# Attention batches of a register loop written out one behind the other

## What is computed

```python
xn = _layernorm(x)                                   # (8, 1024, 256)
Q, K = xn @ Wq, xn @ Wk                              # 16 heads x 2 x 16
V = xn @ Wv                                          # 16 heads x 16
A1 = einsum('bhqd,bhkd->bhqk', Q1, K1) * scaling
A2 = einsum('bhqd,bhkd->bhqk', Q2, K2) * scaling
attn = softmax(A1) - lamb * softmax(A2)
out = einsum('bhqk,bhkd->bhqd', attn, V) @ Wo        # then layer norm, gamma, beta
...
return x + attention(xn) + feed_forward_attention(xn)
```

## Time and profile before

| what | before |
|---|---|
| median of three runs | 4403.33 us |
| the profiled execution | 4398.99 us |
| its span | 4397.2 us |
| TensorE busy | 3937.4 us (90%) |
| VectorE busy | 3106.2 us (71%) |
| ScalarE busy | 2852.8 us (65%) |
| GpSimd busy | 1330.7 us (30%) |
| instructions in the trace | 76116 |
| mean granted TensorE clock | 0.936 |

### The profile page before, as it was taken

How to read it: one execution, slowest core, us unless ns; L and a number is a source line. 1 busy time by engine, 2 the same in 40 slices (tenths; PEclk the granted TensorE clock), 3 DMA queues, 4 the chain that set the end, 5 groups by cost and what they waited for, 6 DMA issues and landing times. The chain is left out here.

```text
span 4397.2 us, 76116 instructions
## 1 busy us (share of the span) xinstructions
PE 3937.4 (90%) x23970; PEld 1611.4 (37%) x23970; DVE 3106.2 (71%) x5547; ACT 2852.8 (65%) x3429; POOL 1330.7 (30%) x1618
## 2 busy tenths in 40 slices
PE   4489999999999999999999999999999477779999
PEld 2123223232322332332223223232322144458888
DVE  3567997888789789878987997888796122234444
ACT  0007887888788788878887887888889444422221
POOL 4211421242142123313221421342141344464330
PEclk7669999999999999999999999999999787789999
DMA  9610211111111111111111111111110366543220
GB/s 317 240 58 28 66 35 50 35 54 45 35 56 62 40 40 54 40 45 40 64 53 32 64 35 50 35 54 52 45 56 24 122 194 200 180 132 96 92 82 20
DMA packets 224807, 332.04 MB, mean 76 GB/s; under 512 B 29297, under 2 KB 165236, under 8 KB 219780
## 3 DMA queue, kind: packets, MB, share of 16 engines
q1 hardware_dynamic: 205956, 276.47, 19.3%
q0 software_dynamic: 18432, 50.36, 3.5%
HBM read 169.34 MB, written 156.34 MB: 74 GB/s over the span
## 5 line engine op out<-in xcount | busy, mean ns | idle before, releaser
L1514 DVE TENSOR_REDUCE arena<-psum 128x1 f32<-128x512 f32 x4096 | 2596.9, 683 | 474.9 <-PE psum L1087 438.8
L1318 ACT ACTIVATE arena<-psum,arena 128x1024 f32<-128x1024 f32 x2048 | 2163.0, 1111 | 193.4 <-PE psum L1125 170.3
L1087 PE MATMUL psum<-arena 48*128 48x512 f16 x4096 | 1383.6, 394 | 80.3 <-DVE arena L1514 22.3
L1141 PE MATMUL psum<-arena 128*32 128x512 f32 x8200 | 1107.3, 612 | 1.4 <-ACT arena L1242 0.7
L1087 PEld LDWEIGHTS psum<-arena 48*128 48x128 f16 x4096 | 322.9, 93 | 1645.0 <-DVE arena L1514 1115.5
L1125 PE MATMUL psum<-arena 50*128 50x512 f16 x4096 | 876.4, 383 | 52.2 <-issue 29.6
L1380 POOL TENSOR_TENSOR arena<-arena 128x16 f32<-128x16 f32 x129 | 28.8, 223 | 1775.6 <-DVE arena L1524 1775.6
L566 DVE TENSOR_TENSOR leaf_arena<-psum,leaf_arena 128x256 f32<-128x256 f32 x240 | 90.7, 420 | 314.8 <-PE psum L510 314.8
L1073 PE MATMUL psum<-arena 128*128 128x256 f32 x1024 | 289.8, 408 | 11.0 <-DVE arena L1514 11.0
L747 ACT ACTIVATE mix_arena<-psum,mix_arena 128x1024 f32<-128x1024 f32 x64 | 71.4, 1115 | 321.9 <-DVE mix_arena L767 321.8
L1125 PEld LDWEIGHTS psum<-arena 50*128 50x128 f16 x4096 | 210.1, 94 | 168.6 <-ACT arena L1318 90.1
(11 more groups left out here) (165 smaller groups left out, 3202.4 us busy)
## 6 DMA issues: line engine op xcount, KB each, us to landing
arena<-scratch_split SPq DMA_DIRECT2D x768, 64.0 KB, 2.1
scratch_split<-arena SPq DMA_DIRECT2D x64, 512.0 KB, 3.2
scratch_sorted_x<-route_arena SPq DMA_DIRECT2D x60, 512.0 KB, 8.1
leaf_arena<-scratch_sorted_x SPq DMA_DIRECT2D x60, 512.0 KB, 4.8
scratch_sorted_y<-leaf_arena SPq DMA_DIRECT2D x60, 512.0 KB, 3.2
leaf_arena<-in_leafw SPq DMA_DIRECT2D x3, 5128.0 KB, 19.2
arena<-in_x SPq DMA_DIRECT2D x18, 512.0 KB, 4.3
scratch_sum<-arena SPq DMA_DIRECT2D x18, 512.0 KB, 3.0
```

The source lines that it names most:

```text
L1087: nc.tensor.matmul(aux_bank[bank], ring[at, slot, 0, m, qt * P:(qt + 1) * P], ring[at, slot, 1, m, c * CH:(c + 1) * CH], start=True, stop=True
L1141: last = nc.tensor.matmul(value_bank[32 * j:32 * j + 32, :], vaug[:, kt, 2 * (s % PER_BATCH) + j % 2, :], prob[:, step % 2, j, :], start=k ...
L1318: nc.scalar.activation(prob[:, step % 2, 2 * h:2 * h + 2, :], score[:, 2 * h:2 * h + 2, :], ACT.Exp, scale=exp_scale[:, s % 2, s // 2:s // ...
L1514: nc.vector.tensor_reduce(halfmax[:, odd, 2 * m + h, qt, c:c + 1], aux_bank[bank], AX.X, ALU.max).then_inc(bank_used[bank], 1)
```

## The change

In each of the five engines' programs the hardware loop and the tail are replaced by a loop of the generating program over eight constants, so that eight bodies are written out one behind the other. The register that held a snapshot of the output group's number on SyncE goes away. Three waits that asked whether their number was a constant now ask whether it is above zero. They stand for the same waits as before: none at the first use, and the same count at every later one. The order of the work on each engine stays as it was.

```diff
--- before.py
+++ after.py
@@ -1021,8 +1021,6 @@
 
                 batch = (i + LAST) % BATCH
                 group = [2 * batch, 2 * batch + 1]
-                if not tail:
-                    group = [sp.snap(group[0]), sp.snap(group[1])]
                 for s in range(PER_BATCH):
 
                     if s % 2 == 0:
@@ -1051,9 +1049,8 @@
                         sp.wait_ge(scattered, i * (16 * TT * NFFF) + 16 * TT * NFFF)
                         load_rows(i + 1)
 
-            with sp.Fori(0, LAST) as i:
-                body(i, False)
-            body(LAST, True)
+            for i in range(BATCH):
+                body(i, i == LAST)
             for h in range(2):
                 sp.wait_ge(groups[h].y_ready, BATCH + 1)
                 groups[h].load(nc.sync, w["x"], 2 * LAST + h)
@@ -1215,9 +1212,8 @@
                             use(i, k + n, s, *todo[n], tail)
                         k += len(todo)
 
-            with pe.Fori(0, LAST) as i:
-                body(i, False)
-            body(LAST, True)
+            for i in range(BATCH):
+                body(i, i == LAST)
             values(LAST, PER_BATCH - 1, STEPS - 1)
             for n, (kind, number) in enumerate(EPILOGUE):
                 bank, turn = bank_use(TAIL + n)
@@ -1244,7 +1240,7 @@
             def read_qk(t, tile, number, bank):
 
                 a, c = number // (QK_UNITS // 2), number % (QK_UNITS // 2)
-                if not (isinstance(t, int) and t == 0):
+                if t > 0:
 
                     act.wait_ge(split_ready, t * 4 + (number // 2 - 3))
                 nc.scalar.activation(rest[:, a, c * QW:(c + 1) * QW], aux_bank[bank][:, 0:QW], ACT.Identity,
@@ -1255,7 +1251,7 @@
                 nc.scalar.activation(vaug[:, tt, :, 0:HD], src, ACT.Copy).then_inc(bank_used[bank], 1)
 
             def read_shift(n, bank):
-                if not (isinstance(n, int) and n == 0):
+                if n > 0:
 
                     act.wait_ge(shift_in, n * 64)
                 nc.scalar.activation(mrow[0:2 * PARTS, :], aux_half[bank][0:2 * PARTS, :], ACT.Copy).then_inc(bank_used[bank], 1)
@@ -1332,9 +1328,8 @@
                             if (s, step) == (1, 2 if h == 0 else 15):
                                 groups[h].guess_std(nc, act, i)
 
-            with act.Fori(0, LAST) as i:
-                body(i, False)
-            body(LAST, True)
+            for i in range(BATCH):
+                body(i, i == LAST)
             copy_values(LAST, PER_BATCH - 1, 1)
             for n, (kind, number) in enumerate(EPILOGUE):
                 act.wait_ge(extra_full, LAST * ITER_EXTRAS + (PRO_EXTRAS + TAIL_EXTRAS + n + 1))
@@ -1352,11 +1347,9 @@
 
                 a, c = number // 2, number % 2
                 cols = slice(c * CH, (c + 1) * CH)
-                if number == 0 and not isinstance(t, int):
+                if number == 0 and t > 0:
 
                     pool.wait_ge(split_stored, t * 32)
-                if isinstance(t, int) and t == 1 and number == 0:
-                    pool.wait_ge(split_stored, 32)
                 nc.gpsimd.tensor_tensor(split[:, a, 0, cols], rest[:, a, cols], zeros[:, 0:CH], ALU.add
                                         ).then_inc(pchain, 1)
                 pool.wait_ge(pchain, t * 4 + (number + 1))
@@ -1426,9 +1419,8 @@
                         for n in range(4 * (s - 1), 4 * s):
                             scatter(n // NFFF, n % NFFF)
 
-            with pool.Fori(0, LAST) as i:
-                body(i, False)
-            body(LAST, True)
+            for i in range(BATCH):
+                body(i, i == LAST)
             join_maps(BATCH * 2 * PER_BATCH, PER_BATCH - 1, 1)
             for h in range(2):
                 groups[h].finish(nc, pool, BATCH)
@@ -1564,9 +1556,8 @@
                             if (s, step) == (1 + h, 4):
                                 groups[h].inverse_std(nc, dve, link, i)
 
-            with dve.Fori(0, LAST) as i:
-                body(i, False)
-            body(LAST, True)
+            for i in range(BATCH):
+                body(i, i == LAST)
             link = Chain(dve, dchain, BATCH * per_iter + links_before)
             wait_read(dve, LAST, TAIL + EPILOGUE.index(("o", 1)))
             invert(1)
```

## The result

The changed kernel takes 4336.47 us in the median of four runs (4331.39 to 4351.24), the kernel before 4404.18 (4395.32 to 4408.93). The ratio is 0.9859, with a 95% interval of 0.9838 to 0.988. The profiled execution takes 4334.91 us, 64.1 less than the profiled one before.

A forecast was written before the change was run, and what follows sets the result against it. TensorE, busy 3937.4 of 4397.2 us, was taken as the bound, VectorE and ScalarE close behind in attention. Savings 50.7 + 6.3 + 4.2 + 2.4 = 63.6 us from 4398.99 gave 4335.4, written 4336; range 4322 to 4348, chance 0.80.

The forecast's parts named there:

- Taken branches: Seams between batches: six taken branches cost 8.45 us each in idle time and lowered clock, 50.7 us saved.
- step 4: Sets 3, 5 and 7 of seven batches: 0.20 us less each without register instructions, 4.2 us saved.
- Set 0 of batch 0: First set, no branch in front: the clock stays low from the stage's start, so nothing credited.
- Sets 1 and 2: Seven loop batches: 3.6 us for registers plus 2.7, half of the longer stretches at 1.2 GHz; 6.3 us saved.
- Sets 4 and 6: Seven batches, priced up to step 12 of set 4: 0.17 us less each, 2.4 us saved.
- Instruction stream: TensorE's program grows from two bodies to eight; code fetch traffic does not grow, zero cost taken.
- Rival B: Written-out batches: straight code stalls at TensorE's code packets, up to +341 us, time 4676; chance 0.03 from its deciding point.
- Rival C: Seams: the branch hides work late in any case, so only registers save 12.9 us, time 4386; chance 0.04.
- Rival A: Attention stage: gaps go but falls to 1.2 GHz come elsewhere; only 41.5 us saved, time 4357; chance 0.12.
- My remark that no stall of the other engines would stay: Seams: other engines stall beside TensorE, but all five loops go together, so none takes its stall's place; no size given.

The follow-up runs named there:

- the paired loop: The kernel before with three loop passes of two batches each, then two batches on constants, on every engine; 4358.18 us, ratio 0.9918.

## Why the prediction was right

The forecast was 4336, the median 4336.47. The steps agree less exactly than that.

1. *Taken branches*: 50.7 us forecast. Before, sets 7 and 0 took 109.85 us around a taken branch; after, 101.13. That is 8.72 a boundary, 52.3 us, of which 1.6 is the register share of set 7 that I had put in step 4. The experiment with registers and no branches gives 54.5 us for the stage. Sets 7 and 0 take 101.51 us in it, so 50.0 us lie at the six boundaries; some 5.0 lie in sets 1 and 2 (729.34 against 724.38), which I had not given to the branches, and the other sets are 0.5 us longer. The mechanism is shown from six sides: the gaps go with the number of taken branches (12, 4, 0), stay when only the others' branches go, lose the second gap with the place of the head, are far shorter for short branches, have a packet of code under way in each of the long ones that were looked at, and the clock of set 0 came back to 1.00 with the gaps gone.

2. *Set 0 of batch 0*: nothing forecast, 0.2 us measured.

3. *Sets 1 and 2*: 6.3 us forecast, -1.5 measured. This is the term that failed.

   Its first part, 0.5 us a batch for registers, came in number (the shortest take 102.85 against 103.41) but not as I read it: set 1 is 0.76 us longer and set 2 1.35 us shorter, with 319 matmuls in set 1 where it had 313, so it is a net of two shifts and not shown to be register time.

   Its second part failed outright. I took the longer stretches at 1.2 GHz for something that would come half as often. By the clock in the traces TensorE is at 1.2 GHz in these sets of the first seven batches for 41.0 us before, 23.9 with registers and no branches, and 58.0 with constants. Three batches are 2.9 us longer than the shortest there and two more 0.8 and 1.3, and it is the same again in a second profile. By one profile of each it is not TensorE's own registers that hold them back: with the other four engines on constants and TensorE on registers there are 61.4 us of it, with TensorE alone on constants 41.0. Nor do registers rule them out, as the paired loop's batch 3 shows. So a form that issues faster can pay for it where TensorE already idles; what decides where and how long a stretch comes is not settled, and the -6.5 us between registers and constants rest on one profile of the one and two of the other. The version where set 1 has neither VectorE's block of statistics nor the second pair of table loads has no such stretch in set 1.

4. *Sets 3, 5, 7*: 4.2 us forecast, 0.20 a set. Set 3 went from 45.41 to 45.22, as forecast; set 7 by 0.27 where no branch is beside it.

5. *Sets 4 and 6*: 2.4 us forecast at 0.17 a set; set 4 as a whole went from 44.92 to 44.68, some 0.25 a set, 3.5 us. The part behind step 12 was left out of the estimate.

6. *Instruction stream*: zero forecast. The queues moved fewer packets than before and no matmul waited by issue. Rival B falls. Rival C falls with the timeline of the seam. Rival A did not come in set 0, where TensorE is at 1.00, but came in part: 17 us more at 1.2 GHz in sets 1 and 2, point 3.

The stage gave 57.6 us where the sum had 63.6: sets 1 and 2 gave 7.8 less, the other terms together 1.8 more. That the time still hit the forecast comes from 6.5 us in stages that the change does not touch, which is luck. My remark that no stall of the other engines would stay was right only since all five loops went: with TensorE alone written out, VectorE's stall took the place.

## What to carry to other kernels

Look for the compare-and-branch at the end of a long hardware loop on each engine, and for idle time by "issue" just behind it, and compare a seam with a taken branch with one without; here each cost 8 to 9 us, more than half of it idle and the rest clock. Write the loop out on every engine that is within 3 us of being late at the seam, not only on the busiest; here that was shown for TensorE and VectorE, and no engine but TensorE was written out alone. Register arithmetic for waits and addresses cost only 0.2 to 0.3 us in a set of 45 us, so where a body is too long to be written out, fewer passes or another place of the loop's head bring part of the gain.

## What was not expected of the hardware

A taken branch is recorded with some 3.5 us on TensorE but with 45 and 63 ns on ScalarE and VectorE, where the same wait for code shows only as the distance to the next instruction: 2.7 us on ScalarE, 3.0 on VectorE. Not every engine has it, against what I wrote from ScalarE's row alone. GpSimd's branch is followed at once:

```profile
L1429 POOLq COMPARE_BRANCH  x1: 45/45/45, 717.1 to 717.1; - x1
L1429 POOLq FUSED_REGOPS  x1: 50/50/50, 717.4 to 717.4; - x1
```

It is 0.3 us at all six of its taken branches. A pass is 264 instructions in the trace on GpSimd; on SyncE it is 347, with 4.6 to 5.0 us from the branch to the next instruction, on ScalarE 875, on VectorE 1127 and on TensorE 5328. No run varied the length, so that GpSimd's short body is the reason is not shown.

A shift of TensorE's loop by 64 instructions took 14.3 us of idle time from six branches. A taken branch over a few instructions took 0.21 us. And the kernel with fewer register operations had longer stretches at 1.2 GHz in three of seven batches, the same three in two profiles.
